# A recommendation tower on one core: the rounds of sums in a row every eight units, places for sixteen units' products and for three loads of weights

## What is computed

```python
e = jnp.stack([tbl_0[ids[:, 0]], ..., tbl_39[ids[:, 39]]], axis=1)   # 512 x 40 x 64
viW = jnp.einsum('bpd,pde->bpe', e[:, i_idx, :], W)                  # 780 pairs
z = jnp.einsum('bpe,bpe->bp', viW, e[:, j_idx, :])
h = jnp.concatenate([z, dense_ctx], axis=1)
h = jnp.maximum(h @ W_top1 + b_top1, 0.0)
h = jnp.maximum(h @ W_top2 + b_top2, 0.0)
y = h @ W_top3
```

## Time and profile before

| | us |
|---|---|
| median of 3 runs | 405.47 |
| lowest and highest | 403.79 to 409.01 |
| the profiled execution | 403.93 |
| its span on the core | 402.1 |

### The profile page before, as it was taken

One profiled execution on the slowest core, in us unless ns is written; L12 is line 12 of the kernel. 1 busy time (PEld: TensorE's weight loads), 2 busy tenths in 40 slices (PEclk: granted clock), 3 DMA queues, 4 the chain that ended last, 5 costly groups with the idle time before them and its releaser, 6 DMA issues.

```text
span 402.1 us, 4540 instructions
## 1 busy us (share of the span) xinstructions
PE 358.1 (89%) x1784; PEld 124.3 (31%) x1784; DVE 272.5 (68%) x287; ACT 45.4 (11%) x73; POOL 155.1 (39%) x261
## 2 busy tenths in 40 slices
PE   0576878997777876999999999999999999999997
PEld 0342424332212221233332333333333333323342
DVE  4989995674454633667667787878767778787620
ACT  2124201200100003010100012000000000300032
POOL 6888888888888888626260000000000000000000
PEclk9968999998989888699999999999999999999999
DMA  5553621221612321112021100111101100000000
GB/s 178 160 182 99 221 73 22 76 75 24 258 28 71 86 66 46 54 55 75 5 75 54 52 25 29 52 55 52 54 0 54 52 0 2 0 2 0 2 0 0
DMA packets 11447, 24.28 MB, mean 60 GB/s; under 512 B 3857, under 2 KB 3857, under 8 KB 11298
## 3 DMA queue, kind: packets, MB, share of 16 engines
q1 hardware_dynamic: 7330, 19.79, 14.6%
q0 software_dynamic: 4096, 4.20, 5.2%
HBM read 23.98 MB, written 0.00 MB: 60 GB/s over the span
## 4 chain that ended last, share of the span: by engine, by line
PE 84%; DVE 9%; issue 3%; DMA 2%; ACT 1%; SPq 0%; DVEq 0%
PE y_ps L487 45%; PE z_ps L511 24%; DVE one_hot L388 5%; PE t_ps L466 4%; PE y_ps L519 3%; PE t_ps L442 2%; DMA table<-in_small_tables 2%; PE t_ps L457 2%; PE y_ps L494 2%; DVE prod L418 2%; PE y_ps L549 2%; DVE x L397 1%; DVE table_parts L382 1%; PE t_ps L555 0%; ACT x L322 0%
## 5 line engine op out<-in xcount | busy, mean ns | idle before, releaser
L418 DVE TENSOR_TENSOR prod<-y_ps,x 128x1024 f32<-128x1024 f32 x190 | 221.6, 1218 | 90.2 <-PE y_ps L487 71.5
L487 PE MATMUL y_ps<-x,w_sb 64*128 64x512 f32 x760 | 190.5, 628 | 24.0 <-DVE prod L418 10.4
L298 POOL DMA_INDIRECT rows<-in_tbl,ids_sb x128 | 123.7, 967 | 37.3 <-POOL spacer L296 20.3
L487 PEld LDWEIGHTS y_ps<-x,w_sb 64*128 64x128 f32 x760 | 67.1, 189 | 132.9 <-issue 70.4
L511 PE MATMUL z_ps<-prod,selector 128*32 128x512 f32 x780 | 101.0, 636 | 0.0
L511 PEld LDWEIGHTS z_ps<-prod,selector 128*32 128x32 f32 x780 | 21.4, 114 | 74.3 <-issue 46.9
L296 POOL MEMSET spacer<- 128x128 f32 x127 | 30.6, 241 | 16.3 <-PE t_ps L457 16.2
L442 PE MATMUL t_ps<-one_hot,table_parts 128*128 128x512 f32 x56 | 18.0, 473 | 13.6 <-DVE one_hot L388 9.4
L324 ACT ACTIVATE x<-t_ps 128x512 f32<-128x512 f32 x15 | 9.0, 597 | 178.8 <-PE t_ps L457 113.7
L388 DVE TENSOR_SCALAR one_hot<-ids_all,numbers 128x512 fp32r<-128x512 int32 x64 | 28.9, 521 | 0.0
L442 PEld LDWEIGHTS t_ps<-one_hot,table_parts 128*128 128x128 f32 x56 | 12.0, 226 | 20.6 <-issue 12.4
(11 more groups left out here) (36 smaller groups left out, 56.6 us busy)
## 6 DMA issues: line engine op xcount, KB each, us to landing
w_sb<-in_w_units SPq DMA_DIRECT2D x25, 512.0 KB
ids_all<-in_ids_one_hot SPq DMA_DIRECT2D x8, 256.0 KB
table<-in_small_tables SPq DMA_DIRECT2D x8, 256.0 KB
rows<-in_tbl,ids_sb POOLq DMA_INDIRECT x128
w_sb<-in_w SPq DMA_DIRECT2D x1, 1792.0 KB
w_sb<-in_w SPq DMA_DIRECT2D x1, 512.0 KB
ids_sb<-in_ids SPq DMA_DIRECT2D x1, 80.0 KB, 2.1
z_sb<-in_dense_t SPq DMA_DIRECT2D x1, 32.0 KB
```

Source lines behind the costliest of these rows:

```text
L298: pool.indirect_dma_start(rows[:, n % ROW_SLOTS, bt, h * D:(h + 1) * D], None, tables[f], bass.IndirectOffsetOnAxis(ap=ids_sb[:, bt, f:f + ...
L418: dve.tensor_tensor(prod[:, at:at + 2, :], y_ps[:, s % Y_SLOTS], leaf, ALU.mult).then_inc(prod_ready, 1)
L487: ins = pe.matmul(y_ps[:, slot, h, :], w_sb[own, c % W_SLOTS, at:at + P], x[own, m, :], start=True, stop=True)
```

## The change

Two rounds are issued in a row, after every eighth unit, where one stood after every fourth: ROUNDS_TOGETHER = 2 and rounds_at(s), which gives rounds 2(q-1) and 2(q-1)+1 after unit 8q + 2. prod has places for 16 units instead of 12 (64 KB a partition instead of 48), and w_sb three places instead of six (12 KB a partition instead of 24). A load of weights now waits till unit 8 (c - 3) + 7 is multiplied. ScalarE's copies of a full bank follow the pair that fills it.

```diff
-W_SLOTS = 6
+W_SLOTS = 3
 Y_SLOTS = 3
-G_UNITS = 12
+G_UNITS = 16
 ROW_SLOTS = 6
 ROUND = 4
+ROUNDS_TOGETHER = 2
...
-def round_at(s):
-    r, rest = divmod(s - SUM_LAG - (ROUND - 1), ROUND)
-    return r if rest == 0 and r >= 0 else None
+def rounds_at(s):
+
+    q, rest = divmod(s + 1 - SUM_LAG, ROUND * ROUNDS_TOGETHER)
+    return range(ROUNDS_TOGETHER * (q - 1), ROUNDS_TOGETHER * q) if rest == 0 and q > 0 else range(0)
+
+
+SUMMED_ALONG = sum(len(rounds_at(s)) for s in range(STEPS))
...
-                if (r := round_at(s)) is not None and r % BANK_ROUNDS == BANK_ROUNDS - 1:
-                    save_bank(r)
-            for r in range(BANK_ROUNDS - 1, ROUNDS, BANK_ROUNDS):
-                if ROUND * r + ROUND - 1 + SUM_LAG >= STEPS:
-                    save_bank(r)
+                for r in rounds_at(s):
+                    if r % BANK_ROUNDS == BANK_ROUNDS - 1:
+                        save_bank(r)
...
-                if (r := round_at(s)) is not None:
+                for r in rounds_at(s):
                     sum_round(r)
-            for r in range(ROUNDS - 1):
-                if ROUND * r + ROUND - 1 + SUM_LAG >= STEPS:
-                    sum_round(r)
+            assert SUMMED_ALONG == ROUNDS - 1
```

## The result

| | before | changed |
|---|---|---|
| median of 4 runs, us | 405.72 | 411.12 |
| the profiled execution, us | 403.93 | 409.18 |
| its span, us | 402.1 | 407.4 |

The ratio is 1.012, with a 95% interval of 1.0066 to 1.0174; by the medians the changed kernel is slower by 5.4 us. Two later comparisons of the same two kernels, on two different chips, gave 1.0236 (1.0185 to 1.0286) and 1.0212 (1.013 to 1.0293); why they are higher is part of what follows.

What follows compares the result with a forecast made beforehand. TensorE was taken to bound the kernel from about 170 us on. Late pairs +5.5 and early part +2.0 gave +7.5 us: 411.4 on the profiled execution, 413.0 on the median, forecast 412.0, range 402 to 420.

Steps and rivals of the forecast that it cites:

- The joined pair: Late part, units 67 to 194: eight units in a row outrun VectorE; 11.72 us against 10.98, +0.74 us each.
- The pairs with extras: Late pairs that also hold a turn, the transposed unit (L494) or L466 matmuls: from nothing to +0.6 us each.
- the price of a released unit: Units 5 to 8 of a late pair, each released by VectorE, were said to take 1.13 us, not 0.86.
- the lower bound: Late pairs: if a released unit takes 0.86 us instead of 1.13, their total is about +2 us instead of +5.5.
- The upper bound: Late pairs: if products start at their full 1.22 us, their total is +9 us instead of +5.5.
- Round 0: Early part: moved from a wait after unit 6, where it cost nothing, to after unit 10: +1.7 us.
- Units 19 to 26: Early pair, its last part taken over by the slow stretch: +0.2 us of the possible 0.74.
- The slow stretch: From 85 to 167 us, rounds take 9.35 us in place of 5.49; joining changes 0, bounds -1.5 and +3 us.
- Weights and product places: Three weight places and sixteen product places: loads still come in time and products wait no longer, price 0.
- Rival 1: The joins win: VectorE's pace doesn't bind, 23 pairs save 0.34 us each, -6.1 us in all; chance 0.13.
- Rival 2: The clock falls in the pairs' new waits: 436 us if once per pair, 424 in every second; chance 0.09.
- Rival 3: The stretch from 85 to 167 us changes its length by a third, 10 us: 402 or 422; chance 0.16.

Runs made afterwards that it cites:

- the kernel with the places alone: The kernel before, rounds single as before, with sixteen product places and three weight loads: ratio 0.9998 (0.9954 to 1.0042), 401.05 us beside 401.78.
- the kernel with half products: The changed kernel with VectorE's products after unit 66 on 256 of the 512 samples: 194.3 us from the sums after unit 66 to those after 194.

## Why the prediction was right

The forecast was 412.0 us and slower by some 7 us; measured were 411.12 and 5.4.

*The joined pair*, worked out at 11.72 us, took 11.68. The steps hold, but for one: the fifth unit is the first one late, released units follow VectorE at 1.13 us, the pair of rounds takes 3.57 us. The pairs with extras came out as said too: 12.01 us with a turn ahead of unit 7 (said 11.97), +0.4 with a turn ahead of unit 2 (said +0.5), +0.5 with the transposed unit last (said +0.6). The sum was said to be +5.5 and is +5.2.

The step that was misread is the price of a released unit. The 1.13 us at 103.47 are a row's length, which reaches 0.07 us into the next: the round behind it starts at 104.53, 1.06 us later, and the eighth unit of the pair above starts at 331.49 and its sums at 332.55, again 1.06. That is 0.86 us and the 0.20 us that every run of units carries at its start; a wait begins a new run. The 1.13 us between units 5 to 8 are VectorE's pitch. With 1.06 the same working gives 11.65 us for the pair, with 1.13 it gave 11.72, so the slip cost 0.07 us. It did matter for the lower bound: a released unit takes neither 0.86 us nor 1.13. The upper bound was too wide, as VectorE's pitch stayed 1.13. On the Trainium skill's rule ("TensorE: Matmul & The Clock Gate", "The mechanism") the row decided rightly: the weights of a unit that waits for a semaphore come with the release.

*Round 0* was the term that was mis-sized. I counted its 1.7 us of work and took the wait that it left for free. It costs 3.0 us by unit 10: 1.7 of work and, as the pair starts at 58.88 instead of 57.56 us, 1.3 of a clock that falls in or behind the longer wait. With the pairs of units 11 to 26 it is 4.3, where I had 2.0. Units 11 to 18 came out at the 0.1 said. Units 19 to 26 took 1.2 us more, where I had given them 0.2 of the 0.74; on the chip without the stretch they take 0.7 more (12.26 against 11.56), and the other 0.5 is within what this period varies by on the chips with it (11.7 to 13.6 us, whatever the order of the rounds).

*The slow stretch* was counted at 0. That holds within its spread, but its nature I left open and still must: it belongs to some chips and not to others (two that were told apart have it, one has not), and no run here that took something away was on a chip that has it.

*Weights and product places* at nothing: shown by the kernel with the places alone, 0.9998, with 0.3 us in its rows.

*Rival 1* (the joins win) was right on the saving, 0.34 us a pair, and wrong on VectorE; the kernel with half products is what it would have been. *Rival 2* (the clock falls in the new waits) didn't come in the late part: no slice after 180 us reads under 9, with four short waits in a pair. It came where I hadn't looked, at 55 us, in a wait of 3.13 us. *Rival 3* (the stretch changes its length) isn't shown; the stretch varies by as much without any change.

That 412.0 came so near 411.12 is luck in part. The late term was 0.3 us too high and the early one 2.3 too low; the stretch, counted at 0, gave 4.3 back in this pair of profiles, which it also does by chance, and 412.0 starts from a median of three runs (405.47) that lies 1.5 us over the profiled execution; on that execution the sum gave 411.4, and 409.18 were measured. What the prediction had right is the direction, the late term and its mechanism. On the chip without the stretch the same +7.5 gives 374.59 + 7.5 = 382.1 against 384.27; there the clock at 55 us and the 0.9 us of units 27 to 66 are missing from the sum.

## What to carry to other kernels

Joining visits that each cost a switch pays only if the engine behind the buffers keeps pace with the longer run: lay out one period with both engines' pitches and the number of buffers, and see which unit is the first to wait (here the fifth of eight, while four was just covered, with 0.25 us to spare). Before moving work out of a place where its engine waits, count what it did for the clock besides its own time: the wait that it leaves is longer, and what comes after it may run slower, as two units did here, with 1.61 and 1.77 us in place of 1.13.

## What the runs showed of the hardware

- One program takes 373 to 375 us on one chip and 402 to 406 in three comparisons on others. The difference lies between some 85 and 167 us of the span, where other engines get TensorE's results up to 5.0 us after its rows end (6.4 in the third profile of the changed kernel) and the granted clock falls again and again (slices of 8 and 6 in tenths). The cause is open. The 30 us between chips are several times what the change does, so only kernels run on the same chip can be compared here.
- A unit that another engine releases takes 1.06 us to the start of what follows, instead of 0.86, after a stop of some 0.1 us (331.49 to 332.55) as after one of 1.28 (103.47 to 104.53) or 2.21 (54.85 to 55.91).
- With a round more of matmuls ahead of a wait, which made that wait 2.19 us in place of 3.13, the granted clock stayed at the upper level (1.00 in place of 0.66 from 55 to 60 us) and the next sums ended 1.4 us earlier, in one profile.
